# Cross-attention and mixture-of-experts layer: the second layer normalisation computed by GpSimd instead of VectorE

## The reference

```python
def _layernorm(x, axis=-1, eps=1e-05):
    m = jnp.mean(x, axis=axis, keepdims=True)
    v = jnp.var(x, axis=axis, keepdims=True)
    return (x - m) / jnp.sqrt(v + eps)

def xattn(X1, X2, QW, Qb, KW, Kb, VW, Vb):          # 16 tiles of 128 x 256
    q = jnp.einsum('ndl,ed->nle', X1, QW) + Qb
    k = jnp.einsum('ndl,ed->nle', X2, KW) + Kb
    v = jnp.einsum('ndl,ed->nle', X2, VW) + Vb
    attn = jax.nn.softmax(jnp.einsum('nqd,nkd->nqk', q, k), axis=-1)
    return jnp.swapaxes(jnp.einsum('nqk,nkd->nqd', attn, v), -1, -2)

def ffn(x):                                          # 2048 rows of 256, 64 experts, 96 slots each
    scores = softmax(x @ gate_weight.T)
    # the best 3 of 8 groups, in them the best 6 experts; each row goes to its experts' slots
    out = (silu(buf @ Wg.T) * (buf @ Wu.T)) @ Wd.T   # for each expert
    shared = jax.nn.silu(x @ Sg.T) * (x @ Su.T) @ Sd.T
    return weighted_sum(out) + shared

x = x + tanh(g_xattn) * xattn(_layernorm(x), ctx, ...)
x = x + tanh(g_ffn)   * ffn(_layernorm(x), ...)      # this layernorm is the second normalisation
```

## Time and profile before

| what | us |
|---|---|
| median of 3 runs | 446.18 |
| the 3 runs | 444.35, 446.18, 452.14 |
| profiled execution, device time | 446.72 |
| its span in the profile | 445.0 |

### The profile page before, as it was taken

One profiled execution on the slowest core, in us unless ns is written; L12 is line 12 of the kernel. 1 busy time (PEld: TensorE's weight loads), 2 busy tenths in 40 slices (PEclk: granted clock), 3 DMA queues, 4 the chain that ended last, 5 costly groups with the idle time before them and its releaser, 6 DMA issues.

```text
span 445.0 us, 8033 instructions
## 1 busy us (share of the span) xinstructions
PE 356.3 (80%) x1949; PEld 256.6 (58%) x1949; DVE 229.3 (52%) x935; ACT 160.7 (36%) x464; POOL 182.1 (41%) x205
## 2 busy tenths in 40 slices
PE   2779998998997987998785987797867989888630
PEld 1668777786886766875453644454434645555320
DVE  5747886888887784437841222232213232246540
ACT  3566664565664121114332322232313333333100
POOL 3000101011011011053677666676666777777540
PEclk9999998999999886999999988999989899999785
DMA  8799772844001010132987879877969634444498
GB/s 295 254 261 264 209 204 79 240 117 154 29 7 49 29 32 1 48 90 46 258 224 197 234 188 243 217 201 204 218 165 247 153 67 69 74 73 70 66 227 128
DMA packets 32989, 66.03 MB, mean 148 GB/s; under 512 B 6125, under 2 KB 21161, under 8 KB 32967
## 3 DMA queue, kind: packets, MB, share of 16 engines
q1 hardware_dynamic: 18587, 46.26, 33.4%
q0 software_dynamic: 12352, 16.26, 21.3%
q10 hardware_dynamic: 2028, 3.25, 2.3%
HBM read 50.17 MB, written 15.59 MB: 148 GB/s over the span
## 4 chain that ended last, share of the span: by engine, by line
DMA 20%; PE 19%; issue 12%; POOL 9%; DVE 6%; ACT 1%; POOLq 1%; another core or an unknown queue 0%; DVEq 0%; SPq 0%; ACTq 0%
PE bank L340 18%; DMA even_rows<-x_all,sidx_now 9%; DMA x1n<-xn_rows,gidx_now 4%; DMA result<-x_all,sidx_now 3%; POOL result L1566 3%; DMA qk_sb<-xn_rows,gidx_now 2%; POOL ctx_sb L1558 2%; DMA ctx_sb<-xn_rows,gidx_now 1%; DMA w_ring<-even_rows 1%; POOL result L1617 1%; PE bank L576 1%; POOL even_rows L1566 1%; DVE hi_hot L1200 1%; POOL qk_sb L1558 1%; ACT x_all L916 1%
## 5 line engine op out<-in xcount | busy, mean ns | idle before, releaser
L340 PE MATMUL bank<-w_ring,p_sb 128*96 (+1 forms) x256 | 94.1, 492 | 1.2 <-issue 0.6
L1425 DVE TENSOR_TENSOR h_sb<-pt_sb,bank 96x176 f32<-96x176 f32 x64 | 21.2, 332 | 106.5 <-ACT pt_sb L906 88.0
L1548 POOL TENSOR_SCALAR zeros<-zeros,token 128x256 f16<-128x256 f16 x16 | 14.6, 925 | 150.0 <-DVE zeros L1209 150.0
L340 PE MATMUL bank<-d_ring,pt_sb 88*96 (+1 forms) x256 | 69.8, 396 | 1.0 <-DVE pt_sb L1420 0.9
L340 PEld LDWEIGHTS bank<-d_ring,pt_sb 88*96 88x96 f32 x256 | 43.7, 172 | 28.1 <-issue 4.5
L1566 POOL DMA_INDIRECT even_rows<-x_all,sidx_now x32 | 46.2, 1443 | 24.2 <-DMA even_rows<-x_all,sidx_now 14.1
L1566 POOL DMA_INDIRECT result<-x_all,sidx_now x32 | 45.9, 1434 | 16.0 <-issue 6.7
L340 PEld LDWEIGHTS bank<-w_ring,p_sb 128*96 128x96 f32 x256 | 38.4, 170 | 23.7 <-issue 6.5
L916 ACT ACTIVATE x_all<-bank,slot_w 96x256 f32<-96x256 f32 x64 | 30.0, 469 | 46.6 <-PE bank L340 32.0
L906 ACT ACTIVATE pt_sb<-bank 96x176 f32<-96x176 f32 x64 | 20.0, 312 | 54.8 <-PE bank L340 46.1
L901 ACT ACTIVATE p_sb<-bank 128x192 f32<-128x192 f32 x64 | 20.9, 326 | 47.7 <-PE bank L576 40.6
(11 more groups left out here) (168 smaller groups left out, 641.1 us busy)
## 6 DMA issues: line engine op xcount, KB each, us to landing
w_ring<-wgu_in SPq DMA_DIRECT2D x32, 704.0 KB
d_ring<-wd_in SPq DMA_DIRECT2D x32, 352.0 KB
even_rows<-zeros SPq DMA_DIRECT2D x1, 2048.0 KB, 7.7
xn_rows<-xn SPq DMA_DIRECT2D x8, 256.0 KB, 4.9
result<-x_all SPq DMA_DIRECT2D x8, 256.0 KB
w_ring<-even_rows SPq DMA_DIRECT2D x4, 512.0 KB, 6.0
result<-w_ring POOLq DMA_DIRECT2D x4, 512.0 KB, 9.1
ctx_sb<-ctx_in ACTq DMA_DIRECT2D x7, 256.0 KB, 6.8
```

Source lines behind the costliest of these rows:

```text
L340: return pe.matmul(o, lhsT, rhs, start=start, stop=stop, skip_group_check=True)
L1425: dve.tensor_tensor(act_sb[:, b % 2, :], silu_sb[:, b % 2, :], eg_ps[b % 2][:, M:2 * M], ALU.mult)\
L1548: last = pool.tensor_scalar(lo_hot[:, i, :], lo_hot[:, i, :], token1[:, at:at + 1], None, ALU.mult)
```

## The change

The two `tensor_scalar` of `norm2` leave VectorE and are made by GpSimd, with the same operands. GpSimd does pair r-1 of step r and then `weigh_hots(r)`, in one list without a loop. It is released by the semaphore `att_step`, at the value that VectorE's last `newton_update` of the step gives; that semaphore now takes 17 counts a step, since the first of VectorE's two instructions counted on it too. `xn2_ready` is now given by GpSimd. VectorE must not overwrite what GpSimd still reads, so it waits for `xn2_ready` at two new places: before it aggregates the next pair's mean (`mv2`), and before the next `newton_start` (`guess`). In step 1 it also waits for its own last `newton_update` before it computes the shifts of the first normalisation.

```diff
-K_ATT = 18
+K_ATT = 17
...
             def statistics(r, i, at, go, part):
 
                 if part == 1:
+                    if i == 0:
+                        wait_apart(dve, s["xn2_ready"], r, waited)
                     go.settled(waited)
                     go.did(dve.bn_aggr(mv2[:, i, :], stats2[:, i, :]))
...
-            def norm2(r, at, go):
-
-                go.settled()
-
-                wait(dve, s["xt_done"], r)
-                wait(dve, s["xn_saved"], 16 * r)
-                for i in range(2):
...
-                    ins = dve.tensor_scalar(xn2[:, i, :], tile, mv2[:, i, 0:1], guess[:, 4 + i:5 + i],
-                                            ALU.subtract, ALU.mult)
-                    if i == 0:
-                        go.did(ins)
-                    else:
-                        ins.then_inc(s["xn2_ready"], 1)
...
                     go_b.settled()
 
+                    wait_apart(dve, s["xn2_ready"], r - 1, waited)
                     c = slice(4, N + 2) if isinstance(r, int) and r == 1 else slice(4, 6)
...
-                if turn:
-                    norm2(r - 1, at_b, go_b)
-                    if isinstance(r, int) and r == 1:
-                        shifts1(4, N, slice(6, N + 2))
+                if isinstance(r, int) and r == 1:
+                    go_b.settled()
+                    shifts1(4, N, slice(6, N + 2))
...
-            pool.wait_ge(s["fills_in"], 64)
-            for r in range(2, PAIRS + 2):
-                weigh_hots(r)
+            def norm2(r):
+
+                pool.wait_ge(s["att_step"], (r + 1) * K_ATT)
+                wait(pool, s["xt_done"], r)
+                wait(pool, s["xn_saved"], 16 * r)
+                for i in range(2):
+                    last = pool.tensor_scalar(xn2[:, i, :], x_all[:, 2 * r + i, :], mv2[:, i, 0:1],
+                                              guess[:, 4 + i:5 + i], ALU.subtract, ALU.mult)
+                last.then_inc(s["xn2_ready"], 1)
+
+            for r in range(1, PAIRS + 2):
+                if r <= PAIRS:
+                    norm2(r - 1)
+                if r == 2:
+                    pool.wait_ge(s["fills_in"], 64)
+                if r >= 2:
+                    weigh_hots(r)
```

More of the change, by code:

```diff
@@ L1060, in statistics @@
                 go.did(dve.bn_stats(stats2[:, i, :], tile))
-            def norm2(r, at, go):
-                go.settled()
-                wait(dve, s["xt_done"], r)
-                wait(dve, s["xn_saved"], 16 * r)
-                for i in range(2):
-                    tile = x_all[:, at + i, :] if isinstance(at, int) else \
-                        x_all[:, bass.ds(at + i, 1), :].rearrange("p a f -> p (a f)")
-                    ins = dve.tensor_scalar(xn2[:, i, :], tile, mv2[:, i, 0:1], guess[:, 4 + i:5 + i],
-                                            ALU.subtract, ALU.mult)
-                    if i == 0:
-                        go.did(ins)
-                    else:
-                        ins.then_inc(s["xn2_ready"], 1)
             def shared_act(q, m, half, ps):
```

## The result

The changed kernel takes 485.96 us (median of four runs, 477.73 to 489.97), the kernel before beside it 447.9 (four runs). The ratio is 1.077, with a 95% interval of 1.053 to 1.101; it leaves out the runs more than 1.5% above the fastest of their kernel, two of the changed one and one of the kernel before, and the two medians as they stand would give 1.085. It is slower, and outside the predicted range. The profiled execution took 484.73 with a span of 482.6, against 446.72 and 445.0.

What follows compares the result with a forecast made beforehand. The first stage's chain was the bound: VectorE's queue last in odd steps, 1.02 of room in even ones. Step 1 +0.92, three pairs -0.57 and step 8 gave +0.4 on 446.72: 447.1 us, range 442.5 to 456.

Steps and rivals of the forecast that it cites:

- What bounds the kernel: First stage: VectorE's queue ends last in odd steps; gains or losses there reach the end one to one.
- the room of an even step: In even step 6 TensorE's logits are ready 1.02 us before VectorE takes their maximum.
- What goes from VectorE: Two normalisation tiles and the wait ahead of them leave VectorE: 0.9 us a step, 7.2 in 8 steps.
- What comes on GpSimd: GpSimd's new f32 tile costs 0.92 us, as the f16 row; the pair 1.82, plus 0.10 for the semaphore.
- the bounds 0.56 and 1.84: GpSimd tile: 0.56 us from two f32 select halves, up to twice 0.92 for two operations per element.
- The release cost of 0.10: Semaphore from VectorE's last Newton step to GpSimd's first tile: 0.10 us.
- Step by step: First stage's lateness: step 1 +0.92, three step pairs -0.57, step 8 starting at +0.35; about +0.4 us in all.
- The forecast's own lateness of 1.12: In odd step 7 `xn2` is ready at 136.76 instead of 135.64, 1.12 us later.
- Rival 3: GpSimd's second tile waits for both `one_hots`, `xn2` 1.74 us later still: +12.6, 459.3 us; chance 0.13.
- Rival 2: VectorE stands still beside GpSimd's normalisation, losing 0.8 us a step: +6.5, 453.2 us; chance 0.15.
- Rival 1: GpSimd is quicker in f32, 1.1 us for the pair: sum -4.1, 442.6 us; chance 0.20.
- What costs nothing: GpSimd's queue, VectorE's two new waits for `xn2_ready` and SyncE's later save of `xn2` were to cost nothing.

Runs made afterwards that it cites:

- hold and filler: Changed kernel, VectorE waiting for `xn2` before `one_hots`, plus four unread TensorE multiplications ahead of the transposes; 456.64 us, ratio 1.016.
- filler: Changed kernel with eight unread TensorE multiplications ahead of its wait for `xn2`; 466.8 us, start of GpSimd's first index copy (ruler) at 205.2.
- it with filler (184.1): Kernel before the change plus unread TensorE multiplications, one ahead of the transposes and three ahead of the shared block; 448.05 us, ratio 0.997.
- the hold: Changed kernel with VectorE made to wait for `xn2` before `one_hots`; 460.93 us, start of GpSimd's first index copy (ruler) at 200.1.
- a piece of `one_hots`: Changed kernel with each of VectorE's two `one_hots` instructions cut into four of 128 x 384; 490.11 us.
- the spare tiles: Kernel before the change, VectorE still normalising, with GpSimd making the same two tiles into a buffer nobody reads; 460.24 us.

## Why the prediction was wrong

Two steps of it failed: it took TensorE's instruction lengths as fixed, and it took GpSimd's second tile to run on beside `one_hots`. A third, the length of the tile, was mis-sized. The three terms, each as a difference of two ruler values:

| term | from | us |
|---|---|---|
| a pair of 2.5 instead of 0.74, `one_hots` held, clock kept, against the kernel before as it is | hold and filler 192.9, before 188.9 | 4.0 |
| the second tile stands still beside `one_hots` | filler 205.2, hold and filler 192.9 | 12.3 |
| TensorE's lower clock after the long wait | after 221.9, filler 205.2 | 16.7 |

They add up to 33.0 because they are steps along one path; taken in another order they would be split otherwise. The first is the least certain. The kernel before doesn't have its clock kept; against it with filler (184.1) the same pair would cost 8.8, with one fast execution on that side. With the hold, the clock is worth 200.1 - 192.9 = 7.2 only, for a wait of 1.8 instead of 3.6, and 2.0 of these lie ahead of step 1's first tile (33.29 against 31.25), so 5.1 is nearer: the two large terms feed each other.

Point by point:

- **What bounds the kernel.** Right in kind: what is lost in the first stage arrives at the end, and the room of an even step was 1.02. A pair that comes 3.1 to 3.6 later than before is far outside that room, so `xn2` ends last in both kinds of step, and the chain names it in each.
- **What goes from VectorE: 0.9 a step.** Right (`quarter` starts 0.07 behind the start of the last Newton step), and worth nothing, since VectorE then waits 4.0 to 4.8 for the logits.
- **What comes on GpSimd: 0.92 a tile.** The term was mis-sized: 1.23 undisturbed, a third more (within the bounds 0.56 and 1.84). It failed in "I take 0.92, the row that differs least": that row is f16, and has other scalars. The Trainium skill, GPSIMD Engine Reference, section Engine selection, with its rough line rate for one input, is further off still: VectorE takes 0.37 for the tile (half of the pair in the earlier trace rows). The release cost of 0.10 was right: 117.94 + 0.16 = 118.10 to 118.21.
- **Step by step.** It took every length of TensorE as fixed. No term asked what a longer gap does to its clock, though the kernel before already shows 0.91 in a window. Behind a wait of 3.4 to 3.8 the transposes, the logits and the shared block ran at the lower level or partly so (1.11, 1.97 and, in step 5, 4.77 for the 16 that took 3.69). This missing term, 16.7, is half of the loss. Larger gaps cost more: waits of 0.4 to 1.2 with one tile on each engine left the ruler at 188.1, waits of 1.4 to 2.0 with the hold cost 5 to 7. But size alone doesn't decide: with the hold a wait of 1.81 in step 4 had slow transposes behind it, and waits of 1.9 in step 3 and 2.0 in step 7 had none. What decides there stays open. The forecast's own lateness of 1.12 on top of the 0.65 of the earlier trace rows makes 1.8 in odd steps, so even with its own lengths this term need not have been nothing. One reading of this part was off as well: it took the scores as done at 128.70, where the next instruction starts, while their own row ends at 127.75 + 1.11 = 128.86. That moves an even step by less than 0.2 and the forecast by less than 1.
- **Rival 3** (chance 0.13) had the mechanism: the second tile stands for both `one_hots`. Its extra of 1.74 measures 1.44 to 1.94, and its signature, GpSimd's line in the chain before the transposes, is there. But its 459.3 lacked both the dear tile and the clock, and the forecast itself left it out, at a cost of 12.3. It was weighed down by the untouched `es_w`, an instruction of 128 x 2 on VectorE, which says nothing of what stops on GpSimd beside a long one.
- **Rival 2** in its size is out: `one_hots` kept their 0.95, `quarter` was 0.22 to 0.26 in the changed kernel (0.41 with VectorE's own tiles in place), and the second `lo_hot` went to 0.48 in four steps. VectorE isn't what lost. **Rival 1** is out: it had 1.1 for the pair, and undisturbed it took 2.46. Whether the f32, the second operation or the scalars from memory make the tile dearer than the f16 row isn't shown.
- **What costs nothing.** Right for GpSimd's queue (`weigh_hots` starts when the pair is over and nobody waits for it), and for the new waits of VectorE.

The rule of the Trainium skill, SBUF — State Buffer, section Who interferes with whom, that a VectorE instruction with two SBUF inputs contends with a GpSimd one that reads and not with one that only writes, is borne out: tiles +1.94 and +3.54, `memset` beside `one_hots` 0.311 as ever. For the two-port modes the page also lets the first to issue hold the shared pair. For `one_hots` the order of starts in the trace doesn't decide: in step 6 the tile began at 142.37, ahead of `one_hots` at 142.43, in step 5 at 119.47, behind the 119.22, and both times the tile was the one that stood, while `one_hots` never took over 0.952. VectorE's two-input instructions did pay where the tile was already running: `lo_hot` with 0.48 for 0.28, and a piece of `one_hots` with 0.55 for 0.34. Not tried: whether other two-input forms (a `scalar_tensor_tensor` as long as `one_hots`) stop GpSimd as well.

## What to carry to other kernels

Before moving work to GpSimd, list what VectorE runs in that time: a long instruction with two inputs in SBUF, as `one_hots` here, can stop a GpSimd instruction that reads SBUF for its full length, and the work moved is then late by that too. And price a later arrival at TensorE not as its lateness alone: look at what the granted clock does behind the longest gaps that are already there, and test it by multiplications that nobody reads. A row of another type is a bound, not a value, for an engine whose cost by type the trace doesn't show.

## What the runs showed of the hardware

- GpSimd's `tensor_scalar` with two scalars from memory takes 1.23 to 1.27 for 128 x 256 in f32; the f16 `tensor_scalar` with one operation takes 0.92; its `memset` of that size 0.311.
- Beside `one_hots` it stood still for what they still had to run: +1.94 with 2 x 0.95, +3.54 with 2 x 1.75. A tile in its last 0.25 wasn't stopped. `one_hots` lost nothing by it, the short two-input `lo_hot` 0.2 in four of eight steps. Beside one-input forms VectorE is the one that pays: `quarter` 0.41 for 0.22 beside the spare tiles.
- After gaps of 3.4 to 3.8 TensorE ran at half its clock for the logits in steps 2 to 7 and for the transposes in steps 3 to 7; with the gaps filled the granted clock was 1.00 for 160 us on end, and the stage 16.7 us shorter.
